# Transposing two normalised activations by DMA from the ACT queue instead of by TensorE and VectorE

## What is computed

```python
# x: (8, 2048, 1024) f32; per core one (2048, 1024) slice
def attn(x, w_lhs, w_rhs):
    scores = einsum('nsd,ntd->nst', x * w_lhs, x * w_rhs)
    return einsum('nst,ntd->nsd', softmax(scores, axis=2), x)

def ffn(x, w12, w3, sw1, sw2, sw3, router_w, bias):
    shared = silu(x @ sw1.T) * (x @ sw2.T) @ sw3.T            # hidden 4096
    scores = sigmoid(x @ router_w.T)                          # 8 experts
    gates = scores * one_hot(top_k(scores + bias, 2)).sum(-2)
    h1, h2 = split(einsum('td,ehd->teh', x, w12))             # hidden 1024 each
    return shared + einsum('teh,edh->td', silu(h1) * h2 * gates, w3)

x = x + layernorm(attn(layernorm(x), w_lhs, w_rhs))
x = x + layernorm(ffn(layernorm(x), ...))
```

## Time and profile before

| | us |
|---|---|
| three runs | 3231.89, 3226.36, 2941.87 |
| median of these | 3226.36 |
| profiled execution, its own time | 2941.34 |
| its span, slowest core | 2939.8 |
| spans of the 8 cores | 2928.8 to 2939.8 |
| PE busy / DVE busy / ACT busy | 2443.4 / 1104.0 / 440.7 |

### The profile page before, as it was taken

One profiled execution on the slowest core, in us unless ns is written; L12 is line 12 of the kernel. 1 busy time (PEld: TensorE's weight loads), 2 busy tenths in 40 slices (PEclk: granted clock), 3 DMA queues, 4 the chain that ended last, 5 costly groups with the idle time before them and its releaser, 6 DMA issues.

```text
span 2939.8 us, 48338 instructions; the slowest of 8 cores (2928.8 to 2939.8 us)
## 1 busy us (share of the span) xinstructions
PE 2443.4 (83%) x17186; PEld 1661.4 (57%) x17186; DVE 1104.0 (38%) x2263; ACT 440.7 (15%) x1048; POOL 242.5 (8%) x462
## 2 busy tenths in 40 slices
PE   0387887679999999999999858999999999989991
PEld 0123333356766666666666645666666666666660
DVE  3504336342222444444444433222234443444344
ACT  2022222101111111111111121111111111111111
POOL 0000010101110111101110110111101110111000
PEclk9999888899999999999999979999999999999995
DMA  5201126605433554245522572554335522553103
GB/s 152 95 1 45 42 55 142 106 2 87 69 52 54 86 87 67 41 67 87 87 41 47 87 135 67 87 87 65 50 59 87 87 43 45 87 87 59 29 1 114
DMA packets 80732, 204.80 MB, mean 70 GB/s; under 512 B 10537, under 2 KB 10858, under 8 KB 80490
## 3 DMA queue, kind: packets, MB, share of 16 engines
q0 software_dynamic: 65952, 151.11, 33.6%
q1 hardware_dynamic: 14546, 50.61, 5.4%
HBM read 335.91 MB, written 16.84 MB: 120 GB/s over the span
## 4 chain that ended last, share of the span: by engine, by line
PE 71%; DVE 17%; issue 4%; DMA 4%; ACT 2%; DVEq 1%; SPq 0%; POOL 0%; ACTq 0%; POOLq 0%
PE h1p L823 20%; PE outp L753 20%; PE h1p L833 20%; DVE acc L772 7%; PE stp L454 4%; DMA x2r<-x2s 2%; PE aop L481 2%; PE aop L484 2%; PE gatesp L808 1%; ACT s1t L845 1%; DMA xr<-x 1%; DVE Gt L857 1%; DVE t2t L853 1%; DVE Gt L862 1%; DVEq L1003 1%
## 5 line engine op out<-in xcount | busy, mean ns | idle before, releaser
L845 ACT ACTIVATE s1t<-h1p 128x256 f32<-128x256 f32 x768 | 295.8, 385 | 2000.2 <-PE h1p L833 1999.8
L853 DVE TENSOR_TENSOR t2t<-h1p,gb 128x256 f32<-128x256 f32 x512 | 217.6, 425 | 840.4 <-ACT s1t L845 770.7
L753 PE MATMUL outp<-sBw,Gt 128*128 128x512 bf16 x1536 | 394.5, 379 | 84.8 <-DVE acc L772 81.9
L753 PE MATMUL outp<-sAw,Gt 128*128 128x512 bf16 x1536 | 397.5, 381 | 77.3 <-DVE acc L772 73.6
L823 PE MATMUL h1p<-n2fm,sAw 128*128 128x256 bf16 x3072 | 405.1, 276 | 45.5 <-DVE Gt L862 45.5
L833 PE MATMUL h1p<-n2fm,sAw 128*128 128x256 bf16 x3072 | 402.9, 275 | 0.0
L823 PE MATMUL h1p<-n2fm,sBw 128*128 128x256 bf16 x3072 | 399.2, 273 | 0.0
L833 PE MATMUL h1p<-n2fm,sBw 128*128 128x256 bf16 x3072 | 398.1, 273 | 0.0
L823 PEld LDWEIGHTS h1p<-n2fm,sAw 128*128 128x128 bf16 x3072 | 298.9, 99 | 167.0 <-issue 61.8
L823 PEld LDWEIGHTS h1p<-n2fm,sBw 128*128 128x128 bf16 x3072 | 298.3, 98 | 120.5 <-issue 11.2
L833 PEld LDWEIGHTS h1p<-n2fm,sAw 128*128 128x128 bf16 x3072 | 303.1, 99 | 37.4
(11 more groups left out here) (103 smaller groups left out, 1059.6 us busy)
## 6 DMA issues: line engine op xcount, KB each, us to landing
sAw<-w12t POOLq DMA_DIRECT2D x64, 512.0 KB, 17.3
sBw<-w12t POOLq DMA_DIRECT2D x64, 512.0 KB, 16.4
xr<-x SPq DMA_DIRECT2D x48, 512.0 KB, 4.1
sAw<-w3t POOLq DMA_DIRECT2D x64, 256.0 KB, 31.6
sBw<-w3t POOLq DMA_DIRECT2D x64, 256.0 KB, 31.2
x2s<-x2t SPq DMA_DIRECT2D x16, 512.0 KB, 5.3
sAw<-w1t POOLq DMA_DIRECT2D x32, 256.0 KB, 14.8
sAw<-w2t POOLq DMA_DIRECT2D x32, 256.0 KB, 15.5
```

The costliest lines, as they stand in the source:

```text
L753: inst = e.matmul(outp[tt][:, half * 512:(half + 1) * 512], Gt[jj_ % 3][:, tt * P:(tt + 1) * P], w3t_[j_][:, half * 512:(half + 1) * 512], ...
L845: E("scalar", lambda e, jj=jj, v=evv: e.activation(s1t[jj % 2][:], h1p[jj % 2][:, 0:TBLK], ACT.Silu).then_inc(S["s_ev"], 1))
L853: E("vector", lambda e, jj=jj, tb=tb: e.tensor_mul(t2t[jj % 2][:], h1p[jj % 2][:, TBLK:2 * TBLK], gate_b[tb % 2][:]), drain=True)
```

## The change

Both sets of PE transposes and DVE copies are replaced by `dma_start_transpose` instructions, SBUF to SBUF, on the ACT queue, one for each 128x128 piece: again 128 for `n1` and 128 for `n2`. ACT waits for the normalised tile ahead of its 8 transposes. For `n1`, DVE waits once for all 128 ahead of `a_fm`. For `n2`, three semaphores serve the three `n2tm` buffers: DVE waits for the transposes of tile gi-3 ahead of writing `n2tm` of tile gi, and TensorE waits for all ahead of the router. `emit_ntr_one` is called at the same places as before; its 8 DMAs stand in ACT's list ahead of the statistics of the current query tile, and the last 16 ahead of the table load for the sigmoid.

```diff
-        W("tensor", S["s_v"], av)
-        if i == 0:
-            W("tensor", S["s_c"], c_all)
-            W("tensor", S["s_cg"], cg_all)
+        W("scalar", S["s_v"], av)
         for c in range(NCD):
-            k = i * NCD + c
-            if k >= 2:
-                W("tensor", S["s_trd"], k - 1)
-            tv = inc(S["s_tr"])
-            E("tensor", lambda e, i=i, c=c, k=k: e.transpose(
-                ntrB[k % 2][:], n1_tm[i][:, c * P:(c + 1) * P], idnb[:]).then_inc(S["s_tr"], 1))
-            W("vector", S["s_tr"], tv)
-            dv = inc(S["s_trd"])
-            E("vector", lambda e, i=i, c=c, k=k: e.tensor_copy(
-                n1_fm[c][:, i * P:(i + 1) * P], ntrB[k % 2][:]).then_inc(S["s_trd"], 1))
-        tr_after_tile.append(cur(S["s_trd"]))
-
-    E("vector", lambda e: e.drain())
+            inc(S["s_ntB"], 16)
+            E("scalar", lambda e, i=i, c=c: e.dma_start_transpose(
+                out=n1_fm[c][:, i * P:(i + 1) * P],
+                in_=n1_tm[i][:, c * P:(c + 1) * P]).then_inc(S["s_ntB"], 16))
+        tr_after_tile.append(cur(S["s_ntB"]))
+
+    W("vector", S["s_ntB"], cur(S["s_ntB"]))
...
     def emit_ntr_one():
         gi, n2v = ntr_pending.pop(0)
-        W("tensor", S["s_v"], n2v)
+        W("scalar", S["s_v"], n2v)
+        r = gi % 3
         for c in range(NCD):
-            kc = ntr_kc[0]
-            ntr_kc[0] += 1
-            if kc >= 2:
-                W("tensor", S["s_trd"], cur(S["s_trd"]) - 1)
-            tv = inc(S["s_tr"])
-            E("tensor", lambda e, gi=gi, c=c, kc=kc: e.transpose(
-                ntrC[kc % 2][:], n2tm[gi % 3][:, c * P:(c + 1) * P],
-                idnb[:]).then_inc(S["s_tr"], 1))
-            W("vector", S["s_tr"], tv)
-            dv = inc(S["s_trd"])
-            E("vector", lambda e, gi=gi, c=c, kc=kc: e.tensor_copy(
-                n2_fm[c][:, gi * P:(gi + 1) * P], ntrC[kc % 2][:]).then_inc(S["s_trd"], 1))
-        ntr_tr_done[gi] = cur(S["s_tr"])
-        gi_tr.append(cur(S["s_trd"]))
+            inc(s_ntP[r], 16)
+            E("scalar", lambda e, gi=gi, c=c: e.dma_start_transpose(
+                out=n2_fm[c][:, gi * P:(gi + 1) * P],
+                in_=n2tm[gi % 3][:, c * P:(c + 1) * P]).then_inc(s_ntP[gi % 3], 16))
+        ntr_tr_done[gi] = (r, cur(s_ntP[r]))
+        gi_tr.append(None)
...
             if gi >= 3:
-                W("vector", S["s_tr"], ntr_tr_done[gi - 3])
+                r, vv3 = ntr_tr_done[gi - 3]
+                W("vector", s_ntP[r], vv3)
...
+    def wait_n2_all(eng):
+        for r in range(3):
+            W(eng, s_ntP[r], n2_all_tot[r])
...
         if qb == 0:
-            W("tensor", S["s_trd"], n2_all_v)
+            wait_n2_all("tensor")
```

More of the change, by code:

```diff
@@ L195, in build_program @@
              "s_x0 s_x1 s_xr0 s_xr1 s_sp0 s_sp1 s_x2r0 s_x2r1 "
-             "s_out0 s_out1 s_gr0 s_gr1").split()
+             "s_out0 s_out1 s_gr0 s_gr1 s_ntB s_nt0 s_nt1 s_nt2").split()
     S = {n: mksem(n) for n in names}
@@ L205, in build_program @@
     s_grP = [S["s_gr0"], S["s_gr1"]]
+    s_ntP = [S["s_nt0"], S["s_nt1"], S["s_nt2"]]
     cnt = {n: 0 for n in names}
@@ L546, in build_program @@
         emit_ntr_one()
+    n2_all_tot = (cur(S["s_nt0"]), cur(S["s_nt1"]), cur(S["s_nt2"]))
+    def wait_n2_all(eng):
+        for r in range(3):
+            W(eng, s_ntP[r], n2_all_tot[r])
     n2_all_v = cur(S["s_trd"])
@@ L551, in build_program @@
     if debug:
-        W("gpsimd", S["s_trd"], n2_all_v)
+        wait_n2_all("gpsimd")
         for c in range(NCD):
```

## The result

| | before | changed |
|---|---|---|
| median of 8 runs, us | 2942.95 | 3199.94 |
| profiled execution, its own time | 2941.34 | 3200.26 |
| span, slowest core | 2939.8 | 3198.6 |

The ratio is 1.0879 (95% interval 1.0866 to 1.0892): +257 us.

The account below looks back on a forecast made before the run. PE bounds stage D; PE and DVE taking turns bound B, the DVE-ACT epilogue chain C. Terms 119.6 + 65.7 + 1 + 18.5 = +204.8 us on 2941.34 gave 3146 us, +7.0%, chance 0.60; range 3045 to 3250 us.

Parts of the forecast that it names:

- D: The last stage, from 545 us on, PE busy 2100.66 of 2395 us: expected unchanged, only shifted, taken as 0.
- c: Time each DMA transpose holds ACT when issued one behind the other: taken as 1.40 us, bounded by 0.42 and 3.0.
- Stage B: From the first tile's normalisation to `a_fm`: 128 transposes in a row on ACT, 182.2 us instead of 62.57, +119.6 us.
- Stage C, ordinary tiles: Eight DMAs ahead of the tile's square make ACT's loop 19.45 us against 13.48: +5.97 for each of 11 tiles, +65.7 us.
- first tiles of a block: Stage C, three with a transposition: ACT's DMAs run during the matmuls and delay the square +0.3 us each, +1 us.
- The end: End of stage C: the last 16 transposes follow the last Exp, 25.4 us to the router instead of 6.93, +18.5 us.
- Rival 1: All DMA transposes: as cheap as a plain DMA, c = 0.42, giving -31 us, 2911 us; chance 0.08.
- Rival 2: ACT issues at 0.42 us and only the DMA engines take 1.40: +110 us, 3052 us; chance 0.08.
- Rival 3: Weights' traffic slows about 19 + 24 transposes by 1.63 us each: +70 us, 3216 us; chance 0.17.
- Rival 4: Each transpose lands ahead of the next, c = 3.0: +608 us, 3550 us; chance 0.05.
- Rival 5: The instruction moves single 2-byte elements, 30 us each: over 10,000 us; chance 0.02.

## Why the prediction was right or wrong

**What bounds the kernel, and direction: right.** B and C carry the loss, D gives 4 us. The changed kernel is slower by 257 us where 205 were forecast; 3199.9 us lies in the range, 54 us over the forecast.

**The price c = 1.40: wrong in size and in reason.** This is the step of the prediction that failed: the term c stood in the sum at 1.40 us and measured 1.59 us on cores 0, 2, 4 and 6, which set the time. I took it from packets at 0.175 us; the transposes' packets cost 0.017 us, and ten of them on each engine 0.17 us in all. That the wrong row gave a number within 14% of the step is luck. The price is the queue's: 0.47 us for a plain copy of this size, 0.64 more for transposing, 0.26 for the drain of ACT, and 0.22 that stayed without the drain. That every ACT instruction is followed by a drain was known from the code, but the sum left it out. With 0.19 us more for each of 128 + 96 + 16 places the forecast rises by 46 us. The Trainium skill's 1309 ns (VectorE: DVE Perf Modes, section The three transpose paths) is none of the times seen here: 1109 ns on the queue, 1590 or 1440 from one to the next, 2.3 us to landing. Its sum, 3123, was farther off than mine, and it too has no term for the drain.

**Stage B: right in mechanism, with one reading wrong.** The 99.7 us for which PE was idle ahead of the transposes are not "of the stage", which is 62.57 us long: they take in PE's wait from the start of the program. Within the stage PE was busy 25.52 of 63 us, so idle 37.5; that engines wait for each other stands. Of the changed stage nothing is covered: 264.04 - 59.72 = 204.3 us, which is 127 steps of 1.59 and 2.3 for the last to land; 182 were forecast, the gap being c.

**Stage C, ordinary tiles: right.** ACT's loop is 8.25 + 8c: 20.97 by c = 1.59, and 21.03 in the trace. The first tiles of a block, put at +0.3 us each, took 1.7 and 2.6 us more (reciprocals of tiles 4 to 5 and 8 to 9), in keeping with 8 x 0.19 us more of c.

**First tiles of a block: one miscounted.** I reckoned three with a transposition behind ST. But AO(3) follows AO(2) with no ST between, so tile 12 is an ordinary one: 12 and 2, not 11 and 3. That adds 5.7 us at c = 1.40.

**The end: right in kind,** 801.02 - 774.57 = 26.5 us for 25.4.

With c = 1.59 and the miscount put right, the prediction's own sum is 143.9 for B, and for C 12 x 7.49 + 2 x 1.85 (8 x 1.59 from 327.54 on, less 338.41) + 21.5 = 115.1, together +259 us against the span's +258.8. So close a match is partly luck. B is 5.6 us too long by it: the transposes began 3.4 us earlier than 63.11, there are 127 steps and not 128, and the last one lands after 2.3 us and not 3.0. C is 1.6 us too short, and D, taken as 0, added nearly 4 us that no run explains.

**The rivals.** Rival 1 (as cheap as a plain DMA) is out: even a plain DMA costs 0.955 us here. The rule of the Trainium skill behind it (Advanced Engine Details and Errata, section X-Bar Transpose (TRN2): transposes as fast as regular DMAs) doesn't hold for pieces of 32 KB, 1.109 against 0.472 us on the queue; for 256 KB a transpose held the queue 1.25 us, with no plain copy of that kind to compare. Rival 2 (engines, not the issuer) had it the wrong way round. Rival 3 (contention) hardly shows in the changed kernel: the periods under the weights' stream are 21.0 to 22.4 us, and the last 16 take 26.5 us, less than the 27.7 of 16 steps and a landing. It is real for large transposes, and for the last ones on SP. Rival 4: landing is 2.3 us, but the next one doesn't wait for it. Rival 5 is out: a transpose holds the queue 1.109 us, not 30.

## What to carry to other kernels

Price a DMA by what it takes on the queue that issues it, drains included, and ask what stands behind it there: the same 128 transposes cost +113 us on ACT, whose statistics stood behind them, and +7 us on SP, once no load waited ahead of them. Merge pieces before moving them to another engine: eight 128x128 transposes in one DMA were 268 us better than in eight, and eight on TensorE with one copy (2897.8 us) were better than any kernel here that does all of `n1` or `n2` by DMA. One DMA for each tile from SP's queue for all tiles wasn't run. When two engines hand a small piece to and fro, the hand-over is most of the price, and it can be had back without leaving the engines.

## What the runs showed of the hardware

- A DMA transpose of 128x128 bfloat16 between SBUF tiles takes 1.109 us on ACT's queue (cores 0, 2, 4, 6) or 1.093 us, lands after 2.3 us (median) and makes 160 packets of 0.017 us; one of 128x1024 held the queue 1.25 us when the DMA engines were otherwise idle, and up to 10.9 us (core 2) beside the weights' stream.
- Behind a DMA on ACT's queue with a drain, the next starts 0.48 us after its end on cores 0, 2, 4 and 6, and 0.35 us on 1, 3, 5 and 7, for transposes and plain copies alike; without the drain the difference between the cores is 0.04 us in the step. Why the cores differ stays open: no run tells what the drain waits for there.
- A DVE copy of 128x1024 bfloat16 from PSUM took 0.69 us, against eight of 128x128 at 0.22 us each.
